# Dimensions transposed three at a time, layer 0's field copies loaded from DRAM and copied into PSUM by ACT

## What is computed

```
e = stack([tbl_f[ids[:, f]] for f in range(39)])          # (1024, 39, 16)
x0 = xk = e
for W, b in ((w0, b0), (w1, b1), (w2, b2)):               # W: (39, fields of xk, 128)
    z = relu(einsum('bhd,bkd,hks->bsd', x0, xk, W) + b)
    xk, direct part = z[:, :64], z[:, 64:]                # the last layer: all 128 direct
logit = sum over d of the direct parts                    # (1024, 256)
y = relu(relu([logit, dense_ctx] @ W1 + b1) @ W2 + b2) @ W3
```

## Time and profile before

| | us |
|---|---|
| three runs | 1267.36 median (1265.43 to 1268.89) |
| profiled execution, its own time | 1268.23 |
| its span, first to last instruction | 1266.4 |
| mean granted TensorE clock | 0.984 |
| DMA moved | 234.42 MB, mean 185 GB/s |

### The profile page before, as it was taken

One profiled execution on the slowest core, in us unless ns is written; L12 is line 12 of the kernel. 1 busy time (PEld: TensorE's weight loads), 2 busy tenths in 40 slices (PEclk: granted clock), 3 DMA queues, 4 the chain that ended last, 5 costly groups with the idle time before them and its releaser, 6 DMA issues.

```text
span 1266.4 us, 15522 instructions
## 1 busy us (share of the span) xinstructions
PE 1231.7 (97%) x4256; PEld 783.5 (62%) x4256; DVE 1165.7 (92%) x1045; ACT 707.7 (56%) x741; POOL 900.8 (71%) x569
## 2 busy tenths in 40 slices
PE   4879999999999999999999999999999999999999
PEld 2446666666666666666666666666666666666664
DVE  7479999989999999999999999999999999999991
ACT  1245655556565655556655655557555565565552
POOL 7676777876878787787877778787878755654540
PEclk7789999999999999999999999999999999999999
DMA  7699878777998888888988888889888888897510
GB/s 210 151 167 222 202 180 187 180 196 191 219 213 178 185 190 197 201 200 210 215 178 185 192 193 201 203 210 219 177 181 195 194 200 198 206 219 174 134 51 0
DMA packets 135922, 234.42 MB, mean 185 GB/s; under 512 B 16403, under 2 KB 25101, under 8 KB 135787
## 3 DMA queue, kind: packets, MB, share of 16 engines
q1 hardware_dynamic: 84335, 151.67, 52.1%
q10 hardware_dynamic: 41994, 79.99, 24.8%
q0 software_dynamic: 9568, 2.47, 2.1%
HBM read 230.21 MB, written 6.23 MB: 187 GB/s over the span
## 4 chain that ended last, share of the span: by engine, by line
PE 83%; DMA 5%; DVE 4%; POOL 3%; SPq 2%; issue 2%; ACT 1%; DVEq 0%; ACTq 0%; POOLq 0%
PE z_odd L1041 33%; PE z_even L1041 31%; PE z_even L1075 7%; PE z_odd L1075 6%; DMA x_rep<-x_rows 2%; DVE whole L889 2%; DMA x_shift<-x_rows 2%; POOL rest L583 2%; PE whole_psum L1069 1%; DVE whole_psum L889 1%; PE x_odd L1095 1%; POOL gathered L568 1%; PE x_even L1095 1%; SPq L441 1%; DVE rest L906 1%
## 5 line engine op out<-in xcount | busy, mean ns | idle before, releaser
L583 POOL TENSOR_TENSOR rest<-whole,head 128x1024 fp32r<-128x1024 f32 x256 | 611.2, 2398 | 247.8 <-ACT head L701 247.2
L889 DVE TENSOR_TENSOR whole<-x_banks,x_rep 128x1024 f32<-128x1024 f32 x448 | 534.1, 1216 | 35.7 <-ACT x_banks L659 30.7
L701 ACT CAST head<-whole 128x1024 fp32r<-128x1024 f32 x256 | 268.6, 1049 | 159.0 <-DVE whole L889 120.7
L568 POOL DMA_INDIRECT gathered<-in_tbl,idx x299 | 286.7, 959 | 82.2 <-issue 74.1
L701 ACT CAST head<-whole_psum 128x1024 fp32r<-128x1024 f32 x192 | 194.8, 1015 | 142.0 <-DVE whole_psum L889 135.8
L889 DVE TENSOR_TENSOR whole_psum<-x_banks,x_rep 128x1024 f32<-128x1024 f32 x192 | 235.5, 1226 | 5.8 <-DMA x_rep<-x_rows 3.5
L906 DVE TENSOR_TENSOR rest<-whole_psum,head 128x1024 fp32r<-128x1024 f32 x192 | 234.5, 1222 | 0.3 <-ACT head L701 0.3
L1041 PE MATMUL z_odd<-head,w_rest 128*128 128x512 f32 x427 | 198.0, 464 | 3.9 <-POOL rest L583 3.3
L1041 PE MATMUL z_even<-head,w_rest 128*128 128x512 f32 x405 | 186.3, 460 | 1.0 <-DVE rest L906 0.8
L1041 PE MATMUL z_odd<-whole,w_whole 128*128 128x512 f32 x400 | 185.3, 592 | 0.5 <-DVE whole L889 0.5
L1041 PE MATMUL z_odd<-head,w_head 128*128 128x512 f32 x460 | 182.5, 397 | 0.0
(11 more groups left out here) (117 smaller groups left out, 1001.5 us busy)
## 6 DMA issues: line engine op xcount, KB each, us to landing
x_rep<-x_rows ACTq DMA_DIRECT2D x128, 512.0 KB, 11.7
x_rep<-x_rows SPq DMA_DIRECT2D x128, 512.0 KB, 11.7
x_shift<-x_rows SPq DMA_DIRECT2D x93, 546.0 KB
x_rep<-x_rows ACTq DMA_DIRECT2D x32, 384.0 KB
x_rep<-x_rows SPq DMA_DIRECT2D x32, 384.0 KB
x_rep<-x_rows SPq DMA_DIRECT2D x32, 256.0 KB
gathered<-in_tbl,idx POOLq DMA_INDIRECT x299, 7.0
x_rows<-xt_and_ctx SPq DMA_DIRECT2D x32, 78.0 KB
```

The source lines that it names most:

```text
L568: nc.gpsimd.indirect_dma_start(gathered[:, f, :], None, tables[f], bass.IndirectOffsetOnAxis(ap=idx[:, f:f + 1], axis=0)).then_inc(s_gathe ...
L583: nc.gpsimd.tensor_tensor(rest[:, split_slot(product)], whole_slot(product), head[:, split_slot(product)].bitcast(F32), ALU.subtract).then ...
L701: nc.scalar.copy(head[:, split_slot(product)], src).then_inc(s_head, 1)
L889: nc.vector.tensor_tensor(out[0:rows, 0:width, :], xk[0:rows, :].unsqueeze(1).to_broadcast([rows, width, N]), x0, ALU.mult).then_inc(s_pro ...
```

## The change

x0 is turned from now on with up to three dimensions in one transpose. From tile 2 on (`packed`) the 16 dimensions of a block are turned in six transposes, of dimensions 0 to 2, 3 to 5, 6 to 8, 9 to 11, 12 to 14 and 13 to 15, of which a tile makes 2, 1, 1 and 2. `emb` of these blocks is laid out by dimension, one copy (`spread` writes 624 columns instead of 1872), and the source of a transpose is 117 adjacent elements. What comes out are 117 partitions with 3 dimensions, not 3 copies of the fields. ACT copies 128 columns for each transpose to `turned`, and SP stores each dimension from there with two DMAs of 128 columns: eight a tile instead of two. The three copies of x0 that layer 0 needs are loaded from `x_rows` with three DMAs of 78 KB into `x0_rows` (behind the `x_shift` loads on SP's queue), and in the next step ACT copies them to the bank `x0_odd`, ahead of head 2 of layer 1 (X0_AFTER = 2). `turned` and `x0_rows` lie in the part of `emb` that is no longer used. The core of the diff:

```diff
+X0_AFTER = 2
+DIM_GROUPS = ((0, 1), (2,), (3,), (4, 5))
+FIRST_DIM = (0, 3, 6, 9, 12, 13)
...
+        def packed(t):
+            return t.turn is not None or t.first >= AHEAD
+        def stored(t):
+            plain = t.turn is None and t.first < AHEAD + 2
+            return t.count(32, 32) if plain else t.count(32 * DPT, -32 * (DPT - 1) * (AHEAD + 2) + 32 * DPT)
+        def x0_loads(t):
+            return t.turn is not None or t.first > AHEAD
...
-                    now = xt[:, nxt.first % 2, :]
-                    sp.dma_start(source(row, 0, [[N, FIELDS], [1, N]]), now).then_inc(s_stored, 16)
-                    if not first and has_layer0(t):
-                        sp.wait_ge(s_prod, before(t, 0, PAIRS0))
-                    sp.dma_start(source(row, FIELDS, [[N, XROWS - FIELDS], [1, N]]),
-                                 now[0:XROWS - FIELDS, :]).then_inc(s_stored, 16)
+                    if packed(t):
+                        for i in range(DPT):
+                            d = nxt.first % TPB * DPT + i
+                            g = min(d // SPC, DIM // SPC - 1) if d < DIM - 1 else DIM // SPC
+                            rows = (d - FIRST_DIM[g]) * FIELDS
+                            slot = turned[:, g % SPC, :]
+                            sp.dma_start(source(row, 0, [[N, FIELDS], [1, P]], i * P),
+                                         slot[rows:rows + FIELDS, :]).then_inc(s_stored, 16)
+                            if i == DPT - 1:
+                                sp.wait_ge(s_prod, before(t, 0, PAIRS0))
+                            sp.dma_start(source(row, FIELDS, [[N, XROWS - FIELDS], [1, P]], i * P),
+                                         slot[rows:rows + XROWS - FIELDS, :]).then_inc(s_stored, 16)
+                    else:
...
-                    wait(sp, s_stored, nxt.count(32, 32))
+                    wait(sp, s_stored, stored(nxt))
                     for r in range(SPC if has_layer0(t) else 0):
                         src = source(row, r, [[N, FIELDS], [SPC * N, CHUNKS0], [1, N]])
                         sp.dma_start(x_shift[FIELDS * r:FIELDS * (r + 1), :, :], src).then_inc(s_shift, 16)
+                    if x0_loads(nxt):
+                        if packed(t):
+                            wait(sp, s_x0_copied, t.count(1, -1))
+                        for r in range(SPC):
+                            sp.dma_start(x0_rows[FIELDS * r:FIELDS * (r + 1), :],
+                                         source(row, 0, [[N, FIELDS], [1, N]])).then_inc(s_x0_rows, 16)
...
+                    nc.scalar.copy(emb_by_dim, gathered[:].rearrange("p f d -> p d f")).then_inc(s_emb, 1)
...
+                    nc.scalar.copy(turned[0:ROWS0, first:first + count, :],
+                                   x0_bank[0][0:ROWS0, 0:count * P].rearrange("p (g b) -> p g b", b=P)
+                                   ).then_inc(s_xt, 1)
...
+            def copy_x0(t):
+                nxt = t.plus(1)
+                wait(act, s_x0_rows, nxt.count(16 * SPC, -16 * SPC * AHEAD))
+                act.wait_ge(s_prod, before(t.plus(-1), 0, PAIRS0))
+                nc.scalar.copy(x0_bank[1][0:ROWS0, :], x0_rows[0:ROWS0, :]).then_inc(s_x0_copied, 1)
...
+                    if n == X0_AFTER and has_layer0(t) and x0_loads(t.plus(1)):
+                        copy_x0(t)
...
-                    dve.wait_ge(s_xt, nxt.count(1, 1))
+                    if x0_loads(nxt):
+                        wait(dve, s_x0_copied, nxt.count(1, -AHEAD))
+                    else:
+                        dve.wait_ge(s_xt, nxt.count(1, 1))
...
-                    out = x0_bank[nxt.first % 2]
-                    for i in range(DPT):
+                    if packed(t):
+                        wait(pe, s_xt, nxt.count(1))
+                    out = x0_bank[0 if packed(t) else nxt.first % 2]
+                    for i, g in enumerate(DIM_GROUPS[nxt.first % TPB] if packed(t) else ()):
+                        rows = emb[:, 0, FIRST_DIM[g] * FIELDS:(FIRST_DIM[g] + SPC) * FIELDS]
+                        mm = nc.tensor.transpose(out[0:ROWS0, i * P:(i + 1) * P], rows, ident[:])
+                    for i in range(0 if packed(t) else DPT):
```

More of the change, by code:

```diff
@@ L160, in build_kernel @@
         emb = sb("emb", [P, SPC, FIELDS * DIM])
+        emb_by_dim = emb[:, 0, :].rearrange("p (d f) -> p d f", f=FIELDS)
+        free_of_emb = emb[:, 1:SPC, :].rearrange("p r q -> p (r q)")
+        x0_rows = free_of_emb[:, 0:N]
+        turned = free_of_emb[:, N:N + SPC * P].rearrange("p (g b) -> p g b", b=P)
         xt_and_ctx = sb("xt_and_ctx", [HALF + CTX, 2, N])
@@ L259, in build_kernel @@
         s_xt = sem("xt_ready")
+        s_x0_rows = sem("x0_rows_loaded")
+        s_x0_copied = sem("x0_copied")
         s_stored = sem("x_rows_stored")
@@ L394, in by_two, with source @@
             return [[0, HALF], [2 * N, repeated(g)], [1, N]]
-        def source(row, first, pattern):
-            return bass.AP(tensor=row.tensor, offset=row.offset + first * N, ap=pattern)
+        def source(row, first, pattern, column=0):
+            return bass.AP(tensor=row.tensor, offset=row.offset + first * N + column, ap=pattern)
         def steps(eng, body, turns=TURNS):
@@ L534, in body @@
                     wait(sp, s_xt, nxt.count(1, 1))
-                    now = xt[:, nxt.first % 2, :]
-                    sp.dma_start(source(row, 0, [[N, FIELDS], [1, N]]), now).then_inc(s_stored, 16)
-                    if not first and has_layer0(t):
-                        sp.wait_ge(s_prod, before(t, 0, PAIRS0))
-                    sp.dma_start(source(row, FIELDS, [[N, XROWS - FIELDS], [1, N]]),
-                                 now[0:XROWS - FIELDS, :]).then_inc(s_stored, 16)
+                    if packed(t):
[11 more added lines that the diff above has]
+                    else:
+                        now = xt[:, nxt.first % 2, :]
+                        sp.dma_start(source(row, 0, [[N, FIELDS], [1, N]]), now).then_inc(s_stored, 16)
+                        if not first and has_layer0(t):
+                            sp.wait_ge(s_prod, before(t, 0, PAIRS0))
+                        sp.dma_start(source(row, FIELDS, [[N, XROWS - FIELDS], [1, N]]),
+                                     now[0:XROWS - FIELDS, :]).then_inc(s_stored, 16)
                     if first:
@@ L681, in load_odd_rows @@
                 row = x_rows[nxt.count(1)] if nxt.turn is None else x_rows[bass.ds(nxt.count(1), 1)]
-                act.wait_ge(s_stored, nxt.count(32, 32))
+                if 0 in groups:
+                    wait(act, s_stored, stored(nxt))
                 for g in groups:
@@ L729, in transposed @@
                 act.wait_ge(s_x0, nxt.count(1, 1))
+                if packed(t):
+                    wait(act, s_stored, stored(nxt.plus(-1)))
+                    groups = DIM_GROUPS[nxt.first % TPB]
+                    first, count = groups[0] % SPC, len(groups)
+                    nc.scalar.copy(turned[0:ROWS0, first:first + count, :],
+                                   x0_bank[0][0:ROWS0, 0:count * P].rearrange("p (g b) -> p g b", b=P)
+                                   ).then_inc(s_xt, 1)
+                    return
                 wait(act, s_stored, nxt.count(32, -32))
@@ L964, in body @@
                         if has_layers12(t):
-                            product(t, 0, j, x0_bank[nxt.first % 2], x_shift[0:ROWS0, c, :], ROWS0)
+                            product(t, 0, j, x0_bank[1 if x0_loads(nxt) else nxt.first % 2], x_shift[0:ROWS0, c, :], ROWS0)
                         else:
```

7 lines of the change are left out of this document (5 added, 2 removed).

## The result

| us | before | after |
|---|---|---|
| median of 19 runs each | 1266.3 (1262.5 to 1268.9) | 1270.1 (1267.6 to 1274.4) |
| ratio, 95% interval | | 1.0031 (1.0021 to 1.0040) |
| profiled execution, its span | 1268.2, 1266.4 | 1268.3, 1266.4 |

The change costs 4 us, 0.3%. The forecast was 26 us (1293.5), with the right sign and the wrong size.

What follows compares the result with a forecast made beforehand. PE bound the kernel at 36.16 us a tile; the x0 loads would make DMA the bound at 37.15, +0.90 over 29 tiles: 1268.2 + 26.1 = 1294.3, or 1293.5 against the median. Range 1255 to 1318.

Steps and rivals of the forecast that it cites:

- The bound now: Kernel before: PE sets the tile at 36.16 us, with a loop over DMA of 35.85 only 0.3 under it.
- DMA loop: x_shift issue, backlog, g4 of x_rep, last layer 1 products, layer 0, store, next x_shift issue: 26.6 + 9.25 = 35.85 us.
- PE's gain: Transposes on PE: 0.70 us a tile becomes 0.16, so PE's tile is 35.62, a gain of 0.54 in 28 tiles.
- a loop of 37.15: DMA's loop after the change, 26.6 + 9.25 + 1.3 us, against 35.62 of PE: DMA becomes the bound.
- ACT, DVE, SP's issues, the seven early stores: ACT's added copy, DVE's new wait, SP's added issues and seven stores ahead of the wait: each costs nothing.
- Rival D: Small stores served one by one send x_shift out 6 us later in each of 28 tiles: 1435 us, chance 0.05.
- The loads: Three x0 loads behind x_shift, 0.240 MB ahead of g2 to g4 of x_rep: 1.3 us more a tile in DMA's loop.
- The step that failed: Last store, alone behind the wait on layer 0's products: 1.54 us to land, taken as unchanged.
- the loop was closed at g4: DMA's loop was taken through g4 of x_rep, read at DVE's ninth layer 1 product, landing 26.6 us after x_shift's issue.
- A: Rival: faster, the x0 loads find room in idle DMA time; 1256 us, or 1252 at PE's bound; chance 0.19.
- B: Rival: no change, a delay of 0.3 to 0.5 us eats just what PE gains; 1267 us, chance 0.08.

Runs made afterwards that it cites:

- e4: The kernel before with only three more loads of 39 rows of 2 KB a tile behind x_shift, into an unread buffer: 1300.3 us, ratio 1.0226.
- e5: e4 with the second store split, 384 columns ahead of the wait for layer 0's products and 128 behind it: 1279.2 us, ratio 1.0097 to the kernel before.
- e8: The changed kernel with 4 or 5 more transposes a tile whose result nobody reads: 1275.3 us, ratio 1.0063 to the kernel before.
- e1: The changed kernel without its three x0 loads a tile, ACT copying weights instead: 1255.7 us, ratio 0.9892 to the kernel before.
- e6: The changed kernel with the x0 loads issued twice, the second time to an unread buffer: 1304.1 us, ratio 1.0284 to the kernel before.
- e12: The changed kernel with all eight stores ahead of the wait for layer 0's products, loads still behind x_shift: 1257.3 us, ratio 0.9898 to the kernel before.
- e10: The changed kernel with all four stores of rows 39 to 58 behind the wait for layer 0's products: 1309.0 us, ratio 1.0307 to the kernel before.

## Why the prediction was right in its sign and wrong in its size

**In microseconds of the medians**, step by step from before to after:

| step | runs | change |
|---|---|---|
| the loads | e4 against before, +2.26% | +28.7 |
| last store a quarter, the rest early | e5 against e4, -1.29% | -16.4 |
| all else in the change, with PE's shorter transposes | after against e5, -0.66% | -8.4 |
| sum | after against before | +3.9 |

The intervals of e4 and e5 are 0.23% and 0.28% to either side, so the two middle terms are known to some 4 to 5 us. The traces, one execution each, give +1.08, -0.87 and -0.23 a tile, times 29 +31, -25 and -7. So the store's term is somewhere from -16 to -25, and the last one is negative but small; e8 gives PE's transposes some 4 of it.

**The bound now.** Right: PE, at 36.16, with the DMA loop close under it.

**PE's gain.** Right in size: 0.11 a transpose, and PE's own bound 35.65 for 35.62. Half right in "PE's gain is lost in its new idle time": that was the case at a loop of 37.15. At the some 36.2 that it became, part of the gain counts (some 4 of 13.9 in e8), since some tiles are set by DMA and others by PE.

**ACT, DVE, SP's issues, the seven early stores.** Right, all nothing (e1). Rival D fell with it: the store to the `x_shift` issue became shorter. The Trainium skill, "DMA: Bandwidth & Descriptors", section "Bandwidth", calls transfers under 64 KB descriptor-dominated, which would have fed D. Here stores of 20 KB and less, issued 0.5 apart in the early group, held nothing up (e1).

**The loads.** The number is right on the kernel before, +0.90 forecast and 1.08 measured in e4, +26.1 against 28.7, but by another way than the forecast's (below), so in part by luck. In after their landing comes 1.41 behind that of `x_shift` (14.68 against 13.27), for 1.3. The rule of the Trainium skill, same page, section "Why a DMA increments its semaphore by 16 and not by 1", gives 13 of the 16 engines for 39 rows, and the estimate from it was 1.1 to 1.2. The 13 is borne out by the trace: in the tile of the rows above each of the three loads raised its semaphore once, 0.5 to 0.9 after its issue, and the other 39 times, 13 for each, came from 616.32 to 619.59. The time isn't settled: 1.41 lies nearer to 1.3, but as other transfers share the stretch it excludes neither.

**The step that failed** is this one: "The last store still stands alone behind the wait (565.30 to 566.84 with its landing), as before." It stands alone, but it isn't as before: it is one dimension's repeats, 20 rows of 512 bytes, not of 2 KB. I had counted the eight DMAs and not looked at what was left of the one on the path. Its way to the `x_shift` issue fell from 1.54 to 1.26, and `x_shift` landed 0.7 sooner after its issue than with the loads and the large store (13.32 in e5, 14.01 in e4). In the sum a term of -16 (-25 by the traces) is missing beside the +26.

**A second one, smaller:** the loop was closed at g4, as in before's waits. With the loads it closes at g2. From the fifth product to the next `x_shift` issue it is 16.09 (625.53 to 641.62; 15.96 in the mean), and 20.04 + 16.09 = 36.13, just under the 36.23 of a tile; by g4 it would be 26.71 + 8.90 = 35.61. Whoever adds the loads to g4's landing adds 1.3 where 0.22 arrived there, and misses that g2, with more margin before, got 1.89. In e4 the same holds: by g2 it is 20.78 + 16.31 = 37.09, by g4 only 27.08 + 9.18 = 36.26. So e4 met the forecast's 37.15 through g2, with a landing that the forecast hadn't sized: the two errors cancelled.

In the 18 us from the `x_shift` issue on, after moves no more than before (173 GB/s, and 175 in the same tile of before). The lateness is made up behind that: over tiles 7 to 30 the means of before and after are 178 and 176 GB/s in those 18 us, 257 and 299 in the next 4, then 288 and 287. DMA in the tile of the rows above, 604.01 to 622 and 622 to 626:

```profile
DMA packets 1849, 3.12 MB, mean 173 GB/s; under 512 B 229, under 2 KB 359, under 8 KB 1849
q1 hardware_dynamic: 1362, 2.59, 75.0%
q10 hardware_dynamic: 229, 0.46, 12.7%
...
DMA packets 627, 1.16 MB, mean 290 GB/s; under 512 B 51, under 2 KB 65, under 8 KB 627
q10 hardware_dynamic: 309, 0.59, 53.8%
q1 hardware_dynamic: 288, 0.56, 49.8%
```

So the first group behind the added bytes pays for them at the slow rate, and the backlog is worked off at the fast one. It looks as if the number of queues made the rate, q1 nearly alone in the one and q1 (SP's) beside q10 (ACT's) in the other. The kernel before speaks against it, from 543 to 549 and from 24 to 26, at the head of the kernel:

```profile
DMA packets 681, 1.26 MB, mean 209 GB/s; under 512 B 51, under 2 KB 74, under 8 KB 681
q1 hardware_dynamic: 330, 0.64, 54.4%
q10 hardware_dynamic: 311, 0.60, 50.1%
...
DMA packets 273, 0.56 MB, mean 280 GB/s; under 512 B 0, under 2 KB 0, under 8 KB 273
q1 hardware_dynamic: 273, 0.56, 103.4%
```

Both queues side by side moved 209 GB/s there, and q1 alone 280. What sets the two rates is open.

**Rivals A and B.** A had the loads find room behind the engines' idle time; they did not, and e6 shows no room at all. B, no change, had the number within 4 (1267) and the right balance, a delay that eats what PE gains, but neither the store nor g2 in it: its 0.3 to 0.5 were meant for g4.

## What to carry to other kernels

When one transfer on the critical loop is split, look at the piece that stays behind the wait, not at the number of pieces: its landing is what the loop pays for, and moving it off the loop altogether was worth 1.3% (e12 against after), as much as taking the loads out (e1). Added bytes ahead of several transfers do not shift them all alike; test each consumer's margin, the first one's above all. And before a term is summed to a loop, ask what else in the same diff shortens that loop.

## What the runs showed of the hardware that was not expected

With the engines at 9 tenths or more and most packets of 2 KB, the rate is 173 to 209 GB/s in some stretches and 280 to 290 in others (above), and the number of queues at work doesn't tell which. Not explained.

One store of 20 rows of 2 KB ahead of `x_shift`, with the new loads behind it, goes with a landing of `x_shift` 0.7 later than four stores of 20 rows of 512 bytes do (14.01 in e4, 13.37 in e10), at the same bytes. Not explained.

By line, two groups of after (busy, mean ns, idle), and the weight loads of the transposes, from adjacent elements (L1160) and with a stride of 64 bytes (L1164):

```profile
L765 ACT COPY emb<-gathered 128x624 f32<-128x624 f32 x7 | 9.3, 1331 | 0.7
L762 ACT COPY emb<-gathered 128x1872 f32<-128x1872 f32 x1 | 1.7, 1747 | 0.0
...
L1160 PEld LDWEIGHTS x_even<-ident,emb 128*117 128x117 f32 x42 | 7.6, 181 | 10.2 <-issue 10.2
L1164 PEld LDWEIGHTS x_even<-ident,emb 128*117 128x117 f32 x8 | 1.8, 290 | 4.4 <-issue 4.4
```

A third of the columns takes ACT 76% of the time when it reads with that stride: 2.1 ns a column for 0.93. The strided weight load takes 290 ns for 181, and with it a transpose took 0.175 (0.70/4) for 0.11. So the stride, and not only the number of transposes, seems to be part of the 0.70 that PE lost; no run changes it alone.
